# One core of two graph layers: the input x by 16 grouped transfers on one queue, a later bias, single output transfers, and a tile's last quarter transposed behind the norm steps

## The reference

```python
# layer 0
a = adj.astype(x.dtype)
deg = jnp.sum(a, axis=1, keepdims=True)
x1 = a @ x / deg
x = _layernorm(x + (jnp.concatenate([x1, x], axis=1) @ weight + bias))
# layer 1
h = jnp.einsum('ni,oi->no', x, W)
e = (h @ a1)[:, None] + (h @ a2)[None, :]
e = jnp.where(adj == 0, -jnp.inf, e)
x = _layernorm(x + softmax(e, axis=1) @ h)
```

## Time and profile before

| what | value |
|---|---|
| median of 3 runs | 1070.46 us (1069.01 to 1072.35) |
| the profiled execution's own time | 1069.98 us |
| its span, first to last instruction | 1068.2 us |
| PE busy | 1005.0 us (94%) |
| PEld busy | 876.4 us (82%) |
| DVE busy | 677.5 us (63%) |
| ACT busy | 611.6 us (57%) |
| POOL busy | 284.5 us (27%) |
| mean granted TensorE clock | 0.979 |
| DMA | 305.35 MB, 286 GB/s over the span |

### The profile page before, as it was taken

How to read it: one execution, slowest core, us unless ns; L and a number is a source line. 1 busy time by engine, 2 the same in 40 slices (tenths; PEclk the granted TensorE clock), 3 DMA queues, 4 the chain that set the end, 5 groups by cost and what they waited for, 6 DMA issues and landing times.

```text
span 1068.2 us, 22037 instructions
## 1 busy us (share of the span) xinstructions
PE 1005.0 (94%) x8783; PEld 876.4 (82%) x8783; DVE 677.5 (63%) x1599; ACT 611.6 (57%) x630; POOL 284.5 (27%) x277
## 2 busy tenths in 40 slices
PE   4789989889889999999999999999999999999996
PEld 4778867778778888888888888888888888888885
DVE  1566767877767677767676576555544656656654
ACT  1597879888888888888768676757421100000000
POOL 4044534434534344334333322322000000000000
PEclk8889999999999999999999999999999999999999
DMA  9489999999999999999999999999130012222011
GB/s 295 179 340 415 422 421 422 420 423 420 422 421 421 422 417 412 421 420 422 400 391 360 352 342 344 348 324 324 63 127 10 26 61 85 85 85 81 19 39 32
DMA packets 51177, 305.35 MB, mean 286 GB/s; under 512 B 6624, under 2 KB 7904, under 8 KB 17536
## 3 DMA queue, kind: packets, MB, share of 16 engines
q0 software_dynamic: 37472, 270.42, 64.0%
q1 hardware_dynamic: 13136, 33.19, 9.0%
q10 hardware_dynamic: 464, 0.30, 0.1%
HBM read 286.29 MB, written 17.59 MB: 284 GB/s over the span
## 4 chain that ended last, share of the span: by engine, by line
PE 63%; DMA 26%; ACT 6%; issue 2%; DVE 1%; SPq 0%; POOL 0%; ACTq 0%; DVEq 0%
PE ps_agg L344 34%; DMA adj_in<-in_adj_dram,chunk 24%; PE ps_part L344 23%; ACT edges L503 5%; PE ps_y L344 4%; DMA bias<-in_L_gnn_bias_dram 2%; PE ps_h L627 1%; PE ps_h L689 1%; DVE partial L823 0%; PE ps_x1T L682 0%; SPq L380 0%; ACT parts L495 0%; POOL adj_in L1254 0%; DVE edgesT L854 0%; DVE packed L867 0%
## 5 line engine op out<-in xcount | busy, mean ns | idle before, releaser
L344 PE MATMUL ps_agg<-parts,edgesT 128*128 128x257 f16 (+1 forms) x5312 | 617.4, 276 | 31.5 <-DVE edgesT L854 31.5
L344 PEld LDWEIGHTS ps_agg<-parts,edgesT 128*128 128x128 fp8e4 x5312 | 521.5, 99 | 114.8 <-DVE edgesT L854 36.0
L503 ACT ACTIVATE edges<-adj_in 128x2048 fp8e4<-128x2048 int32 x256 | 480.5, 1904 | 61.6 <-DMA adj_in<-in_adj_dram,chunk 59.5
L1254 POOL DMA_INDIRECT adj_in<-in_adj_dram,chunk x256 | 278.4, 1087 | 457.6 <-ACT edges L503 446.1
L854 DVE STREAM_TRANSPOSE edgesT<-edges 128x512 uint32<-128x512 uint32 x256 | 168.0, 691 | 75.0 <-ACT edges L503 74.3
L344 PE MATMUL ps_part<-parts,edgesT 128*128 128x258 f16 x1664 | 194.6, 274 | 0.0
L344 PEld LDWEIGHTS ps_part<-parts,edgesT 128*128 128x128 fp8e4 x1664 | 162.5, 98 | 22.9
L573 ACT ACTIVATE std<-mean_var,eps 128x1 f32<-128x1 f32 x64 | 18.9, 295 | 204.2 <-DVE mean_var L1075 204.2
L867 DVE SCALAR_TENSOR_TENSOR packed<-edgesT,packed 128x2048 uint32<-128x2048 uint32 x48 | 109.8, 2287 | 0.1
L344 PE MATMUL ps_part<-parts,packed 128*128 128x258 f16 x836 | 96.4, 273 | 0.0
L344 PEld LDWEIGHTS ps_part<-parts,packed 128*128 128x128 fp8e4 x836 | 81.6, 98 | 11.9
(11 more groups left out here) (118 smaller groups left out, 638.1 us busy)
## 6 DMA issues: line engine op xcount, KB each, us to landing
adj_in<-in_adj_dram,chunk POOLq DMA_INDIRECT x256
out_dram<-edges SPq DMA_DIRECT2D x60, 64.0 KB, 2.8
partial_sums<-partial SPq DMA_DIRECT2D x13, 258.0 KB
adj_in<-partial_sums SPq DMA_DIRECT2D x13, 258.0 KB, 5.9
packed_adj<-packed SPq DMA_DIRECT2D x3, 1024.0 KB
adj_in<-packed_adj SPq DMA_DIRECT2D x2, 1024.0 KB, 6.5
x_all<-in_x_dram SPq DMA_DIRECT2D x6, 256.0 KB, 16.4
x_all<-in_x_dram POOLq DMA_DIRECT2D x6, 256.0 KB
```

Source lines behind the costliest of these rows:

```text
L344: done = eng.matmul(bank[:, 0:cols], rows[:, n // BYTES, n % BYTES, :], moving[:, n, :], start=(n == first), stop=(n == last))
L503: act.activation(edges[:, r // 2, r % 2, :], adj_in[:, m % SLOTS, :], ACT.Copy, scale=EDGE[t % GROUP], saturate=False).then_inc(s_conv, 1)
L1254: pool.indirect_dma_start(adj_in[:, m % SLOTS, :], None, adj_chunks, bass.IndirectOffsetOnAxis(chunk[:, 0:1], 0), element_offset=first_row ...
```

## The change

It has five parts.

1. x comes as 16 transfers on SP's queue, one a group, each over all 128 partitions with 2 KB pieces: in DRAM 4 stretches of 32 pieces, in `x_all` 128 partitions. There is one semaphore a group. ACT and POOL issue none of x. POOL's first adjacency load waits until group 11 of x has landed.
2. The bias transfer goes from SP's queue (behind x) to ACT's (behind the weight), and DVE adds the bias to the first two groups behind the whole loop over j instead of inside it.
3. In the loop over j, DVE transposes a converted quarter of tile 0 one turn later, the fourth one behind the loop.
4. On DVE, the last quarter of each tile from 1 on is transposed behind `degree`, `residual_lo`, `residual`, `weighted` and `moments` of the tile before.
5. The output of a group is stored by one transfer over 128 partitions instead of four over 32; the last row of the last group by one on SP instead of two on SP and two on ACT.

```diff
-    x_quarters = x.rearrange("(a s b w c) f -> s a w b (c f)", a=NQ, s=QUARTERS, b=NB // QUARTERS, w=QUAD, c=BYTES)
-    out_groups = out.rearrange("(a g w c) f -> g a w c f", a=NQ, w=QUAD, c=BYTES)
+    x_groups = x.rearrange("(a g w c) f -> g a w (c f)", a=NQ, w=QUAD, c=BYTES)
+    out_groups = out.rearrange("(a g w c) f -> g a w (c f)", a=NQ, w=QUAD, c=BYTES)
...
-            for a in (0, 1):
-                sp.dma_start(x_all[QUAD * a:QUAD * (a + 1), 0:BYTES, :].rearrange("p c f -> p (c f)"),
-                             x_quarters[0, a][:, 0, :]).then_inc(s_xfirst, 16)
-            for s in range(QUARTERS):
-                for a in (0, 1):
-                    first = 1 if s == 0 else 0
-                    sp.dma_start(x_all[QUAD * a:QUAD * (a + 1), QBLK * s + BYTES * first:QBLK * (s + 1), :]
-                                 .rearrange("p (b c) f -> p b (c f)", c=BYTES), x_quarters[s, a][:, first:, :])\
-                        .then_inc(s_x[s], 16)
-            sp.dma_start(bias[:, :], b0.rearrange("(o f) -> o f", o=1).to_broadcast([P, F])).then_inc(s_bias, 16)
+            for j in range(GROUPS):
+                sp.dma_start(x_all[:, GROUP * j:GROUP * (j + 1), :].rearrange("p c f -> p (c f)"), x_groups[j])\
+                    .then_inc(s_x[j], 16)
...
                 sp.wait_ge(s_out, last_turn(j) + 1)
-                for a in range(NQ):
-                    sp.dma_start(out_groups[loads[j], a], y_out[QUAD * a:QUAD * (a + 1), j % 4, :, :])\
-                        .then_inc(s_outst[j % 4], 16)
+                sp.dma_start(out_groups[loads[j]], y_out[:, j % 4, :, :].rearrange("p c f -> p (c f)"))\
+                    .then_inc(s_outst[j % 4], 16)
...
             act.dma_start(w0_sb[:, :, :], w0.rearrange("(c p) f -> p c f", p=P)).then_inc(s_const, 16)
+            act.dma_start(bias[:, :], b0.rearrange("(o f) -> o f", o=1).to_broadcast([P, F])).then_inc(s_bias, 16)
...
-                if j == 0:
-                    pe.wait_ge(s_xfirst, 16 * NQ)
-                else:
-                    pe.wait_ge(s_x[j // QUARTERS], 16 * 2)
-                    pe.wait_ge(s_xp[j // QUARTERS], 16 * 2)
+                pe.wait_ge(s_x[j], 16)
...
                 if on(t, 0) and t > 0:
-                    for r in range(NQ):
+                    for r in range(NQ - 1):
                         transpose(t, r)
...
                 if on(t, 1):
                     moments(t - 1)
+                if on(t, 0) and t > 0:
+                    transpose(t, NQ - 1)
...
-                if 0 < j <= AHEAD:
-                    keep_v(j - 1)
-                if j in FIRST_AFTER:
-                    transpose(0, FIRST_AFTER.index(j))
+                if j - 1 in FIRST_AFTER:
+                    transpose(0, FIRST_AFTER.index(j - 1))
+            transpose(0, NQ - 1)
+            for j in range(AHEAD):
+                keep_v(j)
...
-            for s in range(QUARTERS):
-                for a in (2, 3):
...
+            pool.wait_ge(s_x[GROUPS * 3 // 4 - 1], 16)
```

More of the change, by code:

```diff
@@ L199, in bass_two_graph_layers @@
         g_banks = [ps_agg[1], ps_small]
-        s_x = [sem(f"x_upper_landed{s}") for s in range(QUARTERS)]
-        s_xp = [sem(f"x_lower_landed{s}") for s in range(QUARTERS)]
-        s_xfirst = sem("x_first_words_landed")
+        s_x = [sem(f"x_landed{j}") for j in range(GROUPS)]
         s_const = sem("w0_landed")
@@ L367, in weighted_at @@
             return exponents_at(g) + 1
-        ALL_STORED = [16 * NQ * sum(1 for j in range(GROUPS - 1) if j % 4 == s) for s in range(4)]
+        ALL_STORED = [16 * sum(1 for j in range(GROUPS - 1) if j % 4 == s) for s in range(4)]
         @block.sync
         def _(sp):
-            for a in (0, 1):
-                sp.dma_start(x_all[QUAD * a:QUAD * (a + 1), 0:BYTES, :].rearrange("p c f -> p (c f)"),
-                             x_quarters[0, a][:, 0, :]).then_inc(s_xfirst, 16)
-            for s in range(QUARTERS):
-                for a in (0, 1):
-                    first = 1 if s == 0 else 0
-                    sp.dma_start(x_all[QUAD * a:QUAD * (a + 1), QBLK * s + BYTES * first:QBLK * (s + 1), :]
-                                 .rearrange("p (b c) f -> p b (c f)", c=BYTES), x_quarters[s, a][:, first:, :])\
-                        .then_inc(s_x[s], 16)
-            sp.dma_start(bias[:, :], b0.rearrange("(o f) -> o f", o=1).to_broadcast([P, F])).then_inc(s_bias, 16)
+            for j in range(GROUPS):
+                sp.dma_start(x_all[:, GROUP * j:GROUP * (j + 1), :].rearrange("p c f -> p (c f)"), x_groups[j])\
+                    .then_inc(s_x[j], 16)
             sp.dma_start(w1_sb[:, :], w1).then_inc(s_const1, 16)
@@ L437, in _ @@
             sp.wait_ge(s_out, TILES - 1)
-            for a in range(NQ):
-                sp.dma_start(out_groups[loads[j], a, :, 0:GROUP - 1, :],
-                             y_out[QUAD * a:QUAD * (a + 1), j % 4, 0:GROUP - 1, :]).then_inc(s_outl, 16)
+            sp.dma_start(out_groups[loads[j], :, :, 0:(GROUP - 1) * F],
+                         y_out[:, j % 4, 0:GROUP - 1, :].rearrange("p c f -> p (c f)")).then_inc(s_outl, 16)
             sp.wait_ge(s_out, TILES)
-            for a in (0, 1):
-                sp.dma_start(out_groups[loads[j], a, :, GROUP - 1, :],
-                             y_out[QUAD * a:QUAD * (a + 1), j % 4, GROUP - 1, :]).then_inc(s_outl, 16)
+            sp.dma_start(out_groups[loads[j], :, :, (GROUP - 1) * F:GROUP * F], y_out[:, j % 4, GROUP - 1, :])\
+                .then_inc(s_outl, 16)
             for s in range(4):
                 sp.wait_ge(s_outst[s], ALL_STORED[s])
-            sp.wait_ge(s_outl, 16 * 2 * NQ)
+            sp.wait_ge(s_outl, 16 * 2)
             sp.wait_ge(s_flag, 1)
@@ L471, in _ @@
         def _(act):
-            for a in (2, 3):
-                act.dma_start(x_all[QUAD * a:QUAD * (a + 1), 0:BYTES, :].rearrange("p c f -> p (c f)"),
-                              x_quarters[0, a][:, 0, :]).then_inc(s_xfirst, 16)
             act.dma_start(w0_sb[:, :, :], w0.rearrange("(c p) f -> p c f", p=P)).then_inc(s_const, 16)
+            act.dma_start(bias[:, :], b0.rearrange("(o f) -> o f", o=1).to_broadcast([P, F])).then_inc(s_bias, 16)
             act.wait_ge(s_fill, 1)
@@ L574, in _ @@
                     .then_inc(s_std1, 1)
[L576 to L579, removed]
             act.wait_ge(s_flag, 1)
@@ L1086, in rows_out @@
                 if c == 0:
-                    wait(dve, s_outst[j % 4], 16 * NQ * (j // 4))
+                    wait(dve, s_outst[j % 4], 16 * (j // 4))
                 dve.tensor_scalar(y_out[:, j % 4, c, :], z[:, u % 2, :], mean_var[:, u % 2, 0:1],
```

## The result

| | before | after |
|---|---|---|
| median of 6 runs each | 1070.34 us (1069.01 to 1072.58) | 1086.74 us (1086.04 to 1087.09) |
| span of the profiled execution | 1068.2 us | 1085.0 us |

The ratio is 1.0149, with a 95% interval of 1.0136 to 1.0162: the change makes the kernel 16.4 us slower. The prediction had the direction, the mechanism and the range (1083 to 1112), but its likeliest time, 1100, was 13 us too long, and the measured time lies outside the 1090 to 1107 to which it gave 0.68. It is the time of rival 2 (1083 to 1090), which had 0.09.

A forecast was written before the change was run, and what follows sets the result against it. The prediction saw a start chain, then a DMA-bound stage, then PE alone from 406 us; 1069.98 + 29 for the later start + 1.3 for the stores = 1100.3, said as 1100 us, range 1083 to 1112.

The forecast's parts named there:

- rival 2: Loading x: four engines, but faster packets, 78 ns each, 2.5 us a group; first contraction at 71.3, 1083 us; chance 0.09.
- Three stages, and a shift that passes through: Whole kernel: start, DMA-bound stage, PE's work alone from 406 us; a start S us later moves everything behind by S.
- Four engines: Transfers of x: both sides share only an outer count of 4, so each runs on four engines; 3.6 us a group.
- Rival 1: Loading x: grouped transfers use all 16 engines, 0.95 us a group; DMA's early hole closes, 17 us gained, 1053; chance 0.12.
- The price of a packet of x: Loading x: 105 to 119 ns a packet, so 3.6 us a group and group 11 landing at 46.8 us.
- What passes x: Last groups of x: packets alternate with the adjacency's; 64 adjacency packets an engine cost 20.0 us, last group at 80.9.
- From the last group to the first contraction: End of the start: 7.5 us from the last group of x, so the first contraction at 88.5 instead of 59.5.
- The signs: Trace: x spaced 3.6 us, DMA share a quarter until 48, POOL idle till 47, first contraction near 88, PE busy from 435.
- The bias and the transposes are inside the term: Start: gains of some 13 us and 4.5 us are waited for at x, so inside the +29.
- Cost 0 for the last quarter behind the norm steps: Later tiles: PE's inline work and slack under DMA hide the 2.2 us of DVE's norm steps and transpose; cost 0.
- Rival 3: Later tiles: that cover fails, PE idles behind contractions, +12 us, 1112; chance 0.08 with anything worse.
- Stores: Output: no cost before the end; there the last row stands behind the three-row part, +1.3 us, between 0 and +3.

The follow-up runs named there:

- s8: Changed kernel with x read from DRAM as 8 stretches of 16 pieces a group (rows of x permuted): 1058.01 us, ratio 0.9883.
- s128: Changed kernel with x read from DRAM as one stretch of 128 pieces a group (rows of x permuted): 1048.76 us, ratio 0.9798.
- group32: Changed kernel with each group of x by four transfers of 32 partitions, two on SP, two on POOL, without POOL's wait: 1052.55 us, ratio 0.9831.
- p23_alone: Kernel before with only the bias moved to ACT's queue and tile 0's four transposes one turn later: 1053.87 us, ratio 0.985.
- p4_alone: Kernel before with only the last quarter of a tile transposed behind the norm steps of the tile before: 1071.25 us, ratio 1.0005.
- no_gate: Changed kernel without POOL's wait for group 11 of x before its first adjacency load: 1090.61 us, ratio 1.0189.

## Why the prediction was right, and where it was not

**Three stages, and a shift that passes through.** Right to 0.1 us: +16.4 at 75.84, at 422.35 and at 1079.28.

**Four engines.** Right. The prediction called it a choice between two bounds that no row decided; s8 and s128 show it. Rival 1 (1053) is what the same loop gives when the engines are 16: s128 took 1048.8 and group32 1052.6.

**The price of a packet of x: this step was mis-sized.** The prediction took 3.6 us a group, from 105 to 119 ns a packet; it measured 2.56 us, 78 to 82 ns. The 105 ns came from a stretch where q1 shared its engines: the two shares there sum to 105.9% of 16 engines, so packets of the two overlap in time. In after the same packets read 97 ns beside the adjacency (5.8% of 160 engine-us for 96) and 82 alone. How much of the difference is overlap and how much a slower packet, no row separates; either way a row of a queue that has company is no price for the queue alone. Rival 2 had it, from 312 ns for 8 KB; the prediction gave it 0.09. (Nor is 78 the same everywhere: in s8, alone on eight engines, a packet took 89 ns, 449 of them in 5 us.) (Its first contraction of 71.3 was 4.5 us short: 2.8 because group 11 came at 36.4 and not 33.6, and 1.7 behind that, where the adjacency passes x: 30.0 us instead of its 28.3.) Group 11 is transposed at 36.40 instead of 46.8, 10.4 us earlier: 11 groups at 1.04 us less make 11.4, and group 0 came 0.9 us late. This is most of the 12.7 us by which the first contraction was early.

**What passes x.** The one-for-one alternation fits the rows: in the stretch of 50 to 60 us 96 packets of x on four engines are 24 each, 417 ns a packet, and the 33 from group 14 to group 15 took 13.78 us, 418 ns each. (On which engine a packet of q0 ran is not in the rows; its 457 on sixteen are 29 each on average.) From the first data of the adjacency (36.4 + 1.9 = 38.3) to the last group took 30.0 us, predicted 32.2. That this is so near is in part luck. x had 108 packets left on each engine and not 113, at 78 instead of 108 ns: 3.8 us less. And fewer packets of the adjacency passed than the 64 of the prediction, though the ninth load went out at 60.05, while x was still on its way. From 68.3 to 72 us, and from 68.3 to 75, with x all in and the tenth load not yet out, q0 reads:

```profile
...
q0 software_dynamic: 54, 0.38, 24.4%
...
```

```profile
...
q0 software_dynamic: 81, 0.57, 20.2%
...
```

24.4% is four engines, and 0.57 MB are 70 packets of 8 KB: 17 on each of the four that x had held were still in line. Of the 72 of nine loads, then, some 55 had passed: 2.8 us less than 64. These terms make 25.6 us, and it took 30.0. A pair cost 417 to 432 ns instead of 390, which is 1.5 to 2.3 us of the 4.4; the rest is open.

**From the last group to the first contraction.** 75.84 - 68.31 = 7.5, as taken.

**The signs.** A quarter's share of DMA, PE's waits for x and a busy PE from 435 us on came as said (from 440 to 800 us PE is busy 360.0 of 360). The spacing of 3.6 us, POOL idle till 47 and the first contraction near 88 did not: they were 2.56, 37.3 and 75.8, and the last is nearer to rival 2's 71.

**The bias and the transposes are inside the term.** Right in that they gave nothing visible: 16.5 us of start, which p23_alone has in full, were waited for at x. It also means that part 1 costs more than the result shows: 75.84 - 43.01 = 32.8 us at the first contraction.

**Cost 0 for the last quarter behind the norm steps.** Right. The waits of the whole run (total us, times, longest):

```profile
...
DVE rcount L858 <- PE ps_agg L342: 61.7, 38, 3.4
...
POOL adj_in L1229 <- DMA x_all<-in_x_dram: 34.9, 1, 34.9
PE ps_agg L342 <- DVE edgesT L831: 33.1, 24, 3.0
...
PE ps_x1T L597 <- DMA x_all<-in_x_dram: 17.2, 6, 11.0
...
```

and two of them before, PE's and DVE's:

```profile
...
PE ps_agg L344 <- DVE edgesT L854: 31.5, 20, 3.6
...
DVE rcount L881 <- PE ps_agg L344: 24.2, 23, 2.9
...
```

DVE's wait at the start of the norm steps (L858) is longer now, as the order wants it, and PE's wait for DVE is 33.1 us over the run, 1.6 more than before. p4_alone has the same two waits, 61.9 and 34.1, and no cost in time that can be told. Rival 3 is out.

**Stores.** 0.4 us at the end instead of 1.3: the three rows are issued 1.78 us ahead of the last one, which seems to be enough for most of them; how many were left is not shown. With the measured start the sum is 1069.98 + 16.4 + 0.4 = 1086.8, against 1086.74.

## What to carry to other kernels

Before several transfers are joined into one, compare the outermost counts of the two sides: here one transfer with 4 stretches on the DRAM side ran on 4 engines, and the same bytes by transfers of 32 partitions, which were not held to 4, made the kernel 34 us faster. A load of small packets that shares its engines with large ones gets about one through for each of theirs, so here 2 KB for 8 KB: keep its engines clear of large packets until it is in, or put it on all engines. And price a packet from a stretch in which its queue is alone.

## What the runs showed of the hardware that was not expected

- SP is held by its own transfers when only four engines take them: an issue takes 0.5 to 0.75 us at first, mostly 2.44 to 2.5 later (after), and up to 13.5 us when the adjacency's packets pass them (no_gate).
- A packet of 2 KB beside packets of 8 KB costs 432 ns of its engine's time (12 to 20 us of no_gate), where the two alone would be 312 + 78 = 390. The rows of that stretch show that both are longer beside the other: a packet of q0 reads 338 ns (96.9% of 128 engine-us for 367), alone 294, and one of q1 reads 95, alone 82.
- The adjacency's packets were longer than alone not only on the engines of x. In the trace of after, from 50 to 60 us, 19 of 20 packets of 8 KB took over 332 ns, median 372, though x had only four of the sixteen engines; in the trace before, from 62 to 66 us, the median is 309. No run shows why.
- The Trainium skill, page "DMA: Bandwidth & Descriptors", section "Queues, rings and completion order", says that an engine goes round robin over its queues by packets, each typically 9 to 17 descriptors. The round robin agrees with the rows; the grain does not seem to, since what the profile counts as a packet is one row of 2 or 8 KB, and these alternated about one for one (24 packets of x on each of its engines in 10 us).
- Starting the adjacency earlier, while twelve of the sixteen engines were idle (share 26.3%), made the kernel 3.9 us slower (no_gate against after).
